# A gated delta-rule attention with a routed feed-forward: projections k, q, v, z as seven block products, four head groups, tiles of 512 tokens

## The chip, the cores and the metric

The kernel runs on one core of a Trainium2 chip. The metric is device time in microseconds; lower is better. Before the change it took 4070.05 us, the median of three runs (4065.21 to 4073.33).

## What is computed

Input x is 4 sequences of 1024 tokens with 512 features, all in f32. It is layer-normalised and goes two ways; the result is x + s * silu(ffn).

```
xn   = layernorm(x)
qkvz = xn @ w_qkvz.T            # 4096 tokens x 6144 rows: q, k 8 heads x 128; v, z 16 heads x 128
q, k, v = silu(causal_conv4([q, k, v]))      # four taps for each channel
beta, g = sigmoid(b), -exp(A_log) * softplus(a + dt_bias)
q, k = l2norm(q), l2norm(k)     # repeated for the two v heads of each k head
S = S * exp(g); S += k (beta * (v - k S)); o = (q * 128**-0.5) S     # for each token, S 128 x 128
s = (rmsnorm(o * silu(z)) * norm_weight) @ w_out.T
g = silu(where(routed, ffn(xn), xn))          # value/output product, gated mlp with 1408 columns
out = x + s * g
```

## The kernel before, in words

The program has two parts, one after the other. `feed_forward` works through 16 units of 256 tokens. It writes the normalised columns (channels on the partitions) to a scratch tensor in HBM, xt_scratch, and the decay rates and the feed-forward result to others. Its own products already use seven block products.

`attention` then goes through two groups of heads (4 k heads and 8 v heads each). In a group it goes through 4 sequences, and in each through 4 tiles of 256 tokens (32 tiles in all). A tile loads its columns into xtile (two buffers, with three tokens of the tile before, 259 columns) and makes its projections: `pe_product` (L1227) computes one feature of 128 channels in four matmuls over the contraction, weights as the stationary operand and 259 columns moving (L1239), or one z block of 512 columns with the tokens stationary (L1243). An f32 matmul stands in the trace as two records. Products and the score products share three PSUM banks in rotation (bank 0, 1, 3). ScalarE evicts a feature with the fourth tap (`act_lead`, L1262), VectorE adds the other three taps straight from the PSUM bank (`dve_conv`, L1269), and ScalarE takes the silu of four heads at once (L1282); z is evicted with its silu (L1277). Keys and queries are transposed in blocks of 32 by VectorE and through a scratch tensor in HBM, for their norms; keys go back the same way.

A chunk is 128 tokens, a unit is a chunk of one block of four v heads; there are 128 units. For each unit: scores (L1472, L1480), the decay matrix (L1489, L1497), its products with the scores (L1512, L1519), then an f16 triangular inverse in six levels with a correction (L1574 to L1690), which runs for two units side by side on two PSUM banks; then the recurrence: recall of the state, eps, learn, answer (L1699 to L1799), the gate with z and the rms norm (L1806 to L1832), a transpose through HBM, and the output product `pe_out` (L1888) into bank 2. The first group of heads stores its partial output in HBM, the second reads it back, adds its own and finishes.

The order of each engine's instructions is worked out before the program is built by `planned` (L980): a list scheduler over lanes of steps with prices from the table TAKES (L2113), dependences from `after` (L1992), and priority to the step with the longest path behind it. Each engine then runs its list in order and waits on semaphores. SP issues nearly all DMAs in such an order; ScalarE's queue issues the loads of xtile (L147), of decay rows (L142) and of the second group's weights.

Of the kernel before, what the change touches and what calls it, by code (L numbers as in the profile page):

```python
# [24 lines left out]
ALU = mybir.AluOpType  # L25
# [4 lines left out]
P = 128  # L30
# [6 lines left out]
GROUPS = 2  # L37
# [4 lines left out]
W_SPANS = {"k": (0, GK * P), "q": (GK * P, 2 * GK * P), "v": (2 * GK * P, (2 * GK + GV) * P), "z": ((2 * GK + GV) * P, GROWS)}  # L42
PADT = T + HALO
TILE = 256
CPT = TILE // P
WIN = TILE + HALO
# [9 lines left out]
HALF_TILES, HALF_CHUNKS = TILES // GROUPS, CHUNKS // GROUPS  # L56
# [49 lines left out]
def resident(nc, ctx):  # L106

    shapes = {"con": ([P, N_CONST, P], F32), "mask": ([P, N_MASK, P], F16), "nw": ([P, 1], F32), "wt": ([P, KT, GROWS], F32), "xtile": ([P, 2, KT, WIN], F32), "sel": ([P, 2, D], F32),
              "taps": ([P, GROUPS, 4 * GK, TAPS], F32), "gts": ([P, SLOTS, CPT, KINDS, GV], F32), "grows": ([P, 2, HEADS * P], F32)}
    r = {name: ctx.enter_context(nc.sbuf_tensor(name, shape, dtype)) for name, (shape, dtype) in shapes.items()}  # L110
    for name in ("c_in", "wk_in", "wq_in", "wv_in", "wz_in", "small_in", "x_in0", "x_in1", "g_out0", "g_out1", *(f"gt_in{i}" for i in range(SLOTS)), "gr_in0", "gr_in1"):
        r[name] = ctx.enter_context(nc.semaphore("a_" + name))
# [15 lines left out]

def load_weights(sp, r, w_qkvz, g, kind):
    lo, hi = W_SPANS[kind]  # L130
    sp.dma_start(r["wt"][:, :, lo:hi], w_qkvz[:, g * GROWS + lo:g * GROWS + hi].rearrange("(k p) n -> p k n", p=P)).then_inc(r[f"w{kind}_in"], 16)
# [13 lines left out]
def load_columns(sp, r, xt_d, q):  # L145
    b, i = divmod(q % HALF_TILES, TPB)
    sp.dma_start(r["xtile"][:, q % 2], xt_d[:, :, b * PADT + i * TILE:b * PADT + i * TILE + WIN]).then_inc(r[f"x_in{q % 2}"], 16)  # L147


def feed_forward(nc, bank, r, x, x_cols, stat_d, cst, masks, w_qkvz, w_ba, conv_w, dt_bias, a_log, norm_weight,  # L150
# [3 lines left out]
    with ExitStack() as ctx:  # L154
# [10 lines left out]
        both = r["wt"][:].rearrange("p k n -> p (k n)")  # L165
# [13 lines left out]
        KH, PIECES = KT // 2, (0, 3, 7, FT)  # L179
# [15 lines left out]
        o3 = r["xtile"][:, 1].rearrange("p k w -> p (k w)")[:, 256:256 + D].rearrange("p (k c) -> p k c", k=KH)  # L195
# [9 lines left out]
        spare, w = r["xtile"][:, 0].rearrange("p k w -> p (k w)"), NJ * NG  # L205
# [3 lines left out]
        gout = r["xtile"][:, 1].rearrange("p k w -> p (k w)")[:, 0:2 * KINDS * w].rearrange("p (t j g i h) -> p t j g i h", t=2, j=NJ, g=GROUPS, i=KINDS)  # L209
# [4 lines left out]
        names = ["c_in", "r_in", *(f"w_in{e}" for e in range(KT)), "g_in0", "g_in1", "g_in2", "d_in", "set", "z_out", "wvo_ps", "wvo_sb", "cb_ps", "at_sum",  # L214
# [80 lines left out]
        def dve_stats(dve, u):  # L295
            for j in range(NJ):
                dve.wait_ge(s[f"x_in{j}"], 16 * (u + 1))
                if u:
                    dve.wait_ge(s["mvs"], NJ * (u - 1) + j + 1)
# [2075 lines left out]
```

## Time and profile before

| | |
|---|---|
| runs | 4070.05 us median (4065.21 to 4073.33) |
| profiled execution, its own time | span of 4068.1 us from the first to the last instruction; no time around it is given |
| TensorE / VectorE / ScalarE / GpSimd busy | 98% / 77% / 56% / 36% |
| mean granted TensorE clock | 0.995 |
| DMA | 400.9 MB, mean 99 GB/s |

The profile is of one execution. Busy times are unions over time, so a line's busy time can hold the end of a matmul while the next one has started. "Idle before" a group is idle time of its engine, with what ended it.

### The profile page before, as it was taken

Reading aid. Unit: us, or ns where it says so; the run is one execution under the profiler, and the core shown is the slowest. Engines: PE = TensorE matmul, PEld = TensorE weight load, DVE = VectorE, ACT = ScalarE, POOL = GpSimd, SP = SyncE. Lnnn points to the kernel's source line nnn. Section 1 sums busy time; section 2 is a strip of 40 time slices with the busy share of each in tenths; the row PEclk is TensorE's granted clock in tenths of the full one; section 3 lists DMA queues with packets and bytes.
Section 4 is the critical chain, followed back from the end, with each engine's and each line's share of the span. In section 5 each row is a group of like instructions: output and inputs, shape, how many; then the busy total and the mean of one; then the engine's idle time right before and its main releaser. Section 6 shows DMA issues by size and latency. Waiting matters only on the chain. (4 is left out here: it accounts for less than half of the span.)

```text
span 4068.1 us, 83861 instructions
## 1 busy us (share of the span) xinstructions
PE 3999.3 (98%) x29432; PEld 3042.7 (75%) x29432; DVE 3147.1 (77%) x6660; ACT 2279.5 (56%) x5904; POOL 1482.6 (36%) x1744
## 2 busy tenths in 40 slices
PE   7999999999999999999999999999999999999998
PEld 6788787787777777777777777777777777777775
DVE  6766666665588878888888887788888888877885
ACT  2222222222277676666767666766666676666664
POOL 2322232322133334333333333334444444444445
PEclk9999999999999999999999999999999999999999
DMA  5212111110534344434434454444444444454443
GB/s 151 51 34 49 31 43 49 25 49 21 163 94 105 105 110 103 104 101 102 102 97 108 105 144 128 110 129 120 111 119 116 114 125 125 119 131 125 119 107 97
DMA packets 813539, 400.89 MB, mean 99 GB/s; under 512 B 475584, under 2 KB 738752, under 8 KB 813120
## 3 DMA queue, kind: packets, MB, share of 16 engines
q1 hardware_dynamic: 777024, 340.30, 32.1%
q10 hardware_dynamic: 36096, 55.24, 4.9%
q8 instruction: 234, 3.83, 0.4%
q14 instruction: 185, 1.52, 0.1%
HBM read 242.70 MB, written 152.63 MB: 97 GB/s over the span
## 5 line engine op out<-in xcount | busy, mean ns | idle before, releaser
L1239 PE MATMUL bank<-xtile,wt 128*128 128x259 f32 x4096 | 1073.2, 391 | 5.2 <-PEq L764 2.5
L1239 PEld LDWEIGHTS bank<-xtile,wt 128*128 128x128 f32 x4096 | 736.9, 191 | 148.7 <-issue 59.6
L1631 ACT ACTIVATE xyinv<-bank 128x512 f16<-128x512 f32 x768 | 451.7, 590 | 320.2 <-PE bank L1574 317.2
L1888 PE MATMUL bank<-wot,xnt 128*128 128x512 f32 x1024 | 537.6, 611 | 1.1 <-DVE xnt L1847 0.8
L1243 PE MATMUL bank<-wt,xtile 128*128 128x512 f32 x1024 | 521.1, 607 | 0.0
L1607 DVE TENSOR_TENSOR wlev<-bank,mask 128x256 f16<-128x256 f32 x768 | 316.8, 413 | 149.9 <-PE bank L1574 146.1
L548 PE MATMUL bank<-hb,wt 128*128 128x128 f32 x2816 | 376.4, 277 | 8.4 <-DVE part L588 5.7
L1269 DVE SCALAR_TENSOR_TENSOR vraw<-bank,taps,vraw 128x256 f32<-128x256 f32 x768 | 363.3, 476 | 27.3 <-ACT vraw L1262 13.5
L548 PEld LDWEIGHTS bank<-hb,wt 128*128 128x128 f32 x2816 | 350.2, 194 | 17.5 <-issue 7.2
L611 POOL TENSOR_TENSOR hid<-part 128x256 f32<-128x256 f32 x176 | 139.0, 790 | 474.2 <-ACT part L603 474.2
L1574 PEld LDWEIGHTS bank<-xyinv,lth 128*128 128x128 f16 x3584 | 202.1, 98 | 146.2 <-issue 71.6
L1549 POOL TENSOR_TENSOR kend<-ktok,gts 128x256 f32<-128x256 f32 x224 | 136.9, 632 | 464.6 <-issue 464.3
L625 PE MATMUL bank<-wd_sb,hid 128*128 128x512 f32 x704 | 304.8, 592 | 0.0
L1524 POOL TENSOR_TENSOR ltm<-ltm,mask 128x512 f32<-128x512 f32 x128 | 154.7, 1209 | 399.2 <-DVE ltm L1512 399.2
L548 PE MATMUL bank<-hb,comb 128*128 128x128 f32 x2112 | 295.9, 277 | 0.0
L1806 POOL TENSOR_TENSOR tq<-tq,zs 128x512 f32<-128x512 f32 x128 | 175.2, 1369 | 326.6 <-DVE tq L1799 308.5
L1574 PE MATMUL bank<-xyinv,lth 128*128 128x64 f16 (+1 forms) x3584 | 264.0, 197 | 18.0 <-ACT xyinv L1631 15.9
L548 PEld LDWEIGHTS bank<-hb,comb 128*128 128x128 f32 x2112 | 266.9, 194 | 0.0
L1243 PEld LDWEIGHTS bank<-wt,xtile 128*128 128x128 f32 x1024 | 178.1, 191 | 118.1 <-issue 114.8
L1574 PEld LDWEIGHTS bank<-wlev,xyinv 128*128 128x128 f16 x3072 | 169.9, 98 | 127.5 <-issue 87.6
L603 ACT ACTIVATE part<-part 128x256 f32<-128x256 f32 x176 | 73.4, 417 | 332.0 <-DVE part L598 332.0
L625 PEld LDWEIGHTS bank<-wd_sb,hid 128*128 128x128 f32 x704 | 132.5, 190 | 160.7 <-issue 157.1
(217 smaller groups left out, 8609.8 us busy)
## 6 DMA issues: line engine op xcount, KB each, us to landing
v_scratch<-vraw SPq DMA_DIRECT2D x64, 512.0 KB, 3.3
vtok<-v_scratch SPq DMA_DIRECT2D x512, 64.0 KB, 2.2
x_scratch<-tq SPq DMA_DIRECT2D x508, 64.0 KB, 1.8
xnt<-x_scratch SPq DMA_DIRECT2D x508, 64.0 KB, 2.5
grows<-row_scratch ACTq DMA_DIRECT2D x126, 256.0 KB, 3.7
k_scratch<-kraw SPq DMA_DIRECT2D x32, 512.0 KB, 2.6
ktok<-k_scratch SPq DMA_DIRECT2D x256, 64.0 KB, 2.5
b_scratch<-kraw SPq DMA_DIRECT2D x256, 64.0 KB, 1.8
```

The source lines that it names most:

```text
L548: i = pe.matmul(dst, w[:, k, f * P:(f + 1) * P], b[:, k], start=first and k == 0, stop=k == KH - 1, skip_group_check=True)
L611: pool.tensor_tensor(hid[:, f, :].rearrange("p (t c) -> p t c", t=2), part[:, n % 3, 0:2], part[:, n % 3, 2:4], ALU.mult).then_inc(s["hid_ ...
L625: i = pe.matmul(bank[6 + j % 2][:], hid[:, f, j * P:(j + 1) * P], wd_sb[:, f, :], start=(f == 0), stop=(f == FT - 1))
L1239: j = pe.matmul(b_p[:, 0:WIN], wt[:, k, c:c + P], xtile[:, par, k, :], **st)
L1243: j = pe.matmul(b_p[:], xtile[:, par, k, HALO + cc * P:HALO + (cc + 1) * P], w, **st)
L1269: dve.scalar_tensor_tensor(out=acc, in0=shaped(feats[i][0], tile_bank("product", q, prod_of[i])[:, tap:tap + TILE]), scalar=taps[:, group( ...
L1524: pool.tensor_tensor(ltm[:], ltm[:], mask[:, M_NEG, :].unsqueeze(1).broadcast_to([P, HEADS, P]), ALU.subtract).then_inc(s["lti_sb"], 1)
L1574: i = pe.matmul(dst[:, h * cols:(h + 1) * cols], lhsT(h), rhs(h), start=start and h == 0, stop=stop, skip_group_check=True)
L1607: dve.tensor_tensor(wlev[:, lv - 1].rearrange("p h (b t s) -> p h b t s", t=2, s=z)[:, :, :, 0, :], b_inv[p][:, 0:HEADS * P // 2].rearrang ...
L1631: act.activation(dst, b_inv[p][:].rearrange("p (a h b s) -> p a h b s", a=2, h=HEADS, s=z), ACT.Copy).then_inc(s[f"xy_sb{p}"], 1)
L1806: pool.tensor_tensor(tq[:, n % 2], tq[:, n % 2], zs[:, tile % 2, cc, m], ALU.mult).then_inc(s["xf_sb"], 1)
L1888: i = pe.matmul(b_o[:], xnt[:, h], wot[:, h], start=(h == 0), stop=(h == GV - 1))
```

## The change

The groups of heads become four (2 k heads, 4 v heads each), the tiles 512 tokens, so there are again 32 tiles and 128 units, and a unit is a chunk. The projections of a tile are three quads: k and q, v, z. A quad is a product of 512 weight columns, 512 tokens and 512 channels, cut into 2 x 2 blocks of 256 each way, and made by seven products of blocks in place of eight; each of the seven is four matmuls with 256 moving columns. Four sums of weight blocks are formed once a group and kind (VectorE for the first group, GpSimd for the others), four sums of column blocks once a tile (VectorE for the first tile, GpSimd for the others). A quad uses all three rotating banks: P1, P6, P7, P4 accumulate in one, and after each ScalarE copies the bank to one quarter of the result; P2 and P5, P3 go to the other two, and VectorE adds those to the copies. For k, q and v the result stands in an SBUF line, `stage`, of 3 + 512 tokens; GpSimd copies the three tokens of the tile before into it and keeps the last three. The lead tap on ScalarE and three taps on VectorE then read that line, with 512 columns each. z is copied to its place and gets its silu there. The score product moves to bank 2, which the output product uses as well: the scores of unit n wait for the eviction of output n - 4, and output c waits for the scores of unit c + 3.

Columns of a tile come in four DMAs and weights of a kind in four, both now from SP. Partial outputs are stored and read back for three groups (96 chunks). Keys and queries are loaded back in 4 DMAs each and not 8. The zero padding of xt_scratch goes, and several semaphores of the feed-forward part are merged.

```diff
-GROUPS = 2
+GROUPS = 4
-TILE = 256
+TILE = 512
+QUADS = ("kq", "v", "z")
 def load_columns(sp, r, xt_d, q):
-    b, i = divmod(q % HALF_TILES, TPB)
-    sp.dma_start(r["xtile"][:, q % 2], xt_d[:, :, b * PADT + i * TILE:b * PADT + i * TILE + WIN]).then_inc(r[f"x_in{q % 2}"], 16)
+    at = q % GROUP_TILES * TILE
+    for slot, k, side in ((B11, 0, 0), (B21, 1, 0), (B12, 0, 1), (B22, 1, 1)):
+        sp.dma_start(r["xtile"][:, q % 2, slot], xt_d[:, k * KH:(k + 1) * KH, at + side * HTILE:at + (side + 1) * HTILE]).then_inc(r[f"x_in{q % 2}"], 16)
...
+        PX, PY, PW = ("P1", "P6", "P7", "P4"), ("P2",), ("P5", "P3")
+        OPERANDS = {"P1": (A11, B11), "P2": (A12, B21), "P3": (S4, B22), "P4": (A22, T4), "P5": (S1, T1), "P6": (S2, T2), "P7": (S3, T3)}
+        COPIED = ("C11", "C12", "C22", "C21")
+        ADDED = ("C11", "C22", "C12")
...
+        def sum_weights(engine, g, kind):
+            engine.tensor_tensor(w[:, S1], w[:, A21], w[:, A22], ALU.add).then_inc(s["wsum"], 1)
+            engine.wait_ge(s["wsum"], done + 1)
+            engine.tensor_tensor(w[:, S3], w[:, A11], w[:, A21], ALU.subtract).then_inc(s["wsum"], 1)
+            engine.tensor_tensor(w[:, S2], w[:, S1], w[:, A11], ALU.subtract).then_inc(s["wsum"], 1)
+            engine.wait_ge(s["wsum"], done + 3)
+            engine.tensor_tensor(w[:, S4], w[:, A12], w[:, S2], ALU.subtract).then_inc(s["wsum"], 1)
+        def sum_columns(engine, q):
...
+        def pe_quad(pe, t, p, r):
+            b = x_bank(t) if p in PX else y_bank(t) if p in PY else w_bank(t)
+            if r == 0:
+                if p == "P1":
+                    pe.wait_ge(s[f"x_in{par}"], 64 * (q // 2 + 1))
+                    pe.wait_ge(s[f"w{kind}_in"], 64 * (group(q) + 1))
+                    if t:
+                        pe.wait_ge(s["qa_sb"], 3 * (t - 1) + 1)
+                elif p == "P2":
+                    if t:
+                        pe.wait_ge(s["qa_sb"], 3 * t)
+                elif p == "P5":
+                    pe.wait_ge(s["xsum"], 4 * (q + 1))
+                    pe.wait_ge(s["wsum"], 4 * (group(q) * NQ + j + 1))
+                    if t:
+                        pe.wait_ge(s["qc_sb"], 4 * t)
+                elif p == "P3":
+                    pe.wait_ge(s["qa_sb"], 3 * t + 2)
+                else:
+                    pe.wait_ge(s["qc_sb"], 4 * t + PX.index(p))
+            for k in range(KH):
+                if kind == "z":
+                    lhs, rhs = xtile[:, par, right, k, r * P:(r + 1) * P], wt[:, left, k, lo:lo + QCOLS]
+                else:
+                    lhs, rhs = wt[:, left, k, lo + r * P:lo + (r + 1) * P], xtile[:, par, right, k, :]
+                i = pe.matmul(b[:, r * QCOLS:(r + 1) * QCOLS], lhs, rhs, start=p in FIRST and r == 0 and k == 0, stop=k == KH - 1, skip_group_check=True)
...
+        def wait_place(engine, t, part):
+            m = staged(q, j)
+            if m:
+                engine.wait_ge(s["cv"], HALO * side_done(m - 1, side))
+                if half:
+                    engine.wait_ge(s["edge"], edges(m))
...
+        def act_copy(act, t, i):
+            act.activation(target(t, part), pairs(x_bank(t)), ACT.Silu if last_z else ACT.Copy).then_inc(s["qc_sb"], 1)
+        def dve_add(dve, t, i):
+            dve.tensor_tensor(a, pairs(y_bank(t) if part == "C11" else w_bank(t)), a, ALU.add).then_inc(s["qa_sb"], 1)
+        def pool_halo(pool, m):
+                pool.tensor_copy(stage[:, :, :, 0:HALO], tails[:, j]).then_inc(s["edge"], 1)
+        def pool_tail(pool, m):
+            pool.tensor_copy(tails[:, j], stage[:, :, :, TILE:TILE + HALO]).then_inc(s["edge"], 1)
...
         def act_lead(act, q, i):
-            act.activation(feature(q, i), shaped(kind, tile_bank("product", q, prod_of[i])[:, HALO:HALO + TILE]), ACT.Copy, scale=taps[:, group(q), i, HALO:HALO + 1]).then_inc(s["lead"], 1)
+            act.activation(feature(q, i), shaped(kind, stage[:, side, r, HALO:HALO + TILE]), ACT.Copy, scale=taps[:, group(q), f, HALO:HALO + 1]).then_inc(s["lead"], 1)
         def dve_conv(dve, q, i, tap):
-            dve.scalar_tensor_tensor(out=acc, in0=shaped(feats[i][0], tile_bank("product", q, prod_of[i])[:, tap:tap + TILE]), scalar=taps[:, group(q), i, tap:tap + 1], in1=acc,
-                                     op0=ALU.mult, op1=ALU.add).then_inc(s[done[tap + 1]], 1)
+            dve.scalar_tensor_tensor(out=acc, in0=shaped(feats[i][0], stage[:, side, r, tap:tap + TILE]), scalar=taps[:, group(q), f, tap:tap + 1], in1=acc,
+                                     op0=ALU.mult, op1=ALU.add).then_inc(s["cv"], 1)
...
+        def act_zsilu(act, q, part):
+            act.activation(a, a, ACT.Silu).then_inc(s["zs_sb"], 1)
...
         def pe_scores(pe, n):
+            if n > LEAD:
+                pe.wait_ge(s["po_sb"], n - LEAD)
...
         def pe_out(pe, c, h):
+                pe.wait_ge(s["kq_sb"], min(c + LEAD + 1, UNITS))
...
+        def product_order():
+            yield 0, "P1"
+            for t in quads:
+                yield from ((t, p) for p in (("P5", "P2", "P6", "P7") if QUADS[t % NQ] == "v" else ("P5", "P6", "P2", "P7")))
+                if t + 1 in quads:
+                    yield t + 1, "P1"
+                yield from ((t, p) for p in ("P4", "P3"))
...
-            ("act", "lead"): 0.47, ("act", "z"): 0.60, ("act", "silu"): 1.06, ("act", "keys"): 1.27, ("act", "queries"): 1.27,
+            ("act", "lead"): 0.64, ("act", "zsilu"): 0.85, ("act", "silu"): 1.06, ("act", "keys"): 1.27, ("act", "queries"): 1.27,
-            ("dve", "conv"): 0.50,
+            ("dve", "conv"): 0.64,
```

## Rows read from the trace of the kernel before

**Rows 1.** The page: busy us, share of span, instructions, by engine.
```profile
PE 3999.3 (98%) x29432; PEld 3042.7 (75%) x29432; DVE 3147.1 (77%) x6660; ACT 2279.5 (56%) x5904; POOL 1482.6 (36%) x1744
```

**Rows 2.** Busy time by stage: bounds, length, engines busy, granted clock, DMA.
```profile
0.00:1061.00 1061.00, 1036.56 (x6644) 840.42 (x6644) 684.81 (x1691) 254.56 (x599) 299.91 (x402) 0.99 0.20 56
1061.00:1200.00 139.00, 130.25 (x779) 96.30 (x780) 109.51 (x209) 80.75 (x202) 32.97 (x36) 0.96 0.40 112
1200.00:4003.00 2803.00, 2783.32 (x21657) 2074.78 (x21656) 2326.02 (x4707) 1922.50 (x5036) 1126.12 (x1279) 1.00 0.44 114
4003.00:4068.00 65.00, 49.17 (x360) 31.15 (x356) 26.73 (x56) 21.64 (x68) 23.61 (x28) 0.92 0.32 81
```

**Rows 3.** The same for VectorE alone, then for the taps of line 1269.
```profile
1061.00:4003.00 2942.00, 2435.53 (x4914) 1.00 0.44 114
1061.00:4003.00 2942.00, 725.11 (x1536) 1.00 0.44 114
```

**Rows 4.** Lines by shape: the products; busy us, mean ns, idle before.
```profile
L1239 PE MATMUL bank<-xtile,wt 128*128 128x259 f32 x4096 | 1073.2, 391 | 5.2 <-PEq L764 2.5 <-DVE vraw L1269 1.4 <-DVE kqt L1269 1.0
L1243 PE MATMUL bank<-wt,xtile 128*128 128x512 f32 x1024 | 521.1, 607 | 0.0
```

**Rows 5.** Timeline of ScalarE at the start: start, duration, line, idle before.
```profile
1066.67 0.47 ACT L1262 ACTIVATE kraw<-bank,taps 128x256 f32<-128x256 f32 x1 [1.22 <-PE bank L1239]
...
1068.43 0.47 ACT L1262 ACTIVATE kraw<-bank,taps 128x256 f32<-128x256 f32 x1 [1.28 <-PE bank L1239]
...
1101.78 0.60 ACT L1277 ACTIVATE zs<-bank 128x512 f32<-128x512 f32 x1 [2.84 <-PE bank L1243]
...
1105.21 0.60 ACT L1277 ACTIVATE zs<-bank 128x512 f32<-128x512 f32 x1 [2.84 <-PE bank L1243]
```

**Rows 6.** VectorE by line: ns min/median/max, first and last start.
```profile
L1519 DVE TENSOR_TENSOR pt<-gam,kqm x128: 647/682/1764, 1118.7 to 4003.2; 128x512 f32<-128x512 f32 x128
L526 DVE SCALAR_TENSOR_TENSOR h<-h,routed,xn x32: 750/751/1097, 106.4 to 993.2; 128x512 f32<-128x512 f32 x32
L1799 DVE TENSOR_TENSOR tq<-bank,tq x112: 673/684/693, 1203.0 to 4050.5; 128x512 f32<-128x512 f32 x112
L1653 DVE TENSOR_TENSOR errh<-errd,mask x128: 398/415/1370, 1154.9 to 4039.1; 128x512 f16<-128x512 f16 x128
```

**Rows 7.** Lines by shape: two operations with two SBUF inputs.
```profile
L1519 DVE TENSOR_TENSOR pt<-gam,kqm 128x512 f32<-128x512 f32 x128 | 109.9, 859 | 1.0 <-PE bank L1786 1.0
L1653 DVE TENSOR_TENSOR errh<-errd,mask 128x512 f16<-128x512 f16 x128 | 69.6, 544 | 0.0
```

**Rows 8.** Timeline of GpSimd and VectorE in one stretch of attention.
```profile
2522.82 1.15 POOL L1524 TENSOR_TENSOR ltm<-ltm,mask 128x512 f32<-128x512 f32 x1 [9.85 <-DVE ltm L1512]
2523.26 1.00 DVE L1653 TENSOR_TENSOR errh<-errd,mask 128x512 f16<-128x512 f16 x1
```

**Rows 9.** Lines by shape: ScalarE and GpSimd.
```profile
L1262 ACT ACTIVATE vraw<-bank,taps 128x256 f32<-128x256 f32 x256 | 118.9, 468 | 92.1 <-PE bank L1239 90.8
L1532 ACT ACTIVATE lth<-ltm 128x512 f16<-128x512 f32 x128 | 80.5, 629 | 23.0 <-POOL ltm L1524 23.0
L1282 ACT ACTIVATE vraw<-vraw 128x1024 f32<-128x1024 f32 x64 | 67.6, 1056 | 16.0 <-DVE vraw L1269 15.5
L1524 POOL TENSOR_TENSOR ltm<-ltm,mask 128x512 f32<-128x512 f32 x128 | 154.7, 1209 | 399.2 <-DVE ltm L1512 399.2
```

**Rows 10.** DMA issues: line, count, size, us to landing.
```profile
xtile<-xt_scratch ACTq DMA_DIRECT2D x30, 518.0 KB, 4.3
```

**Rows 11.** Timeline at the start of attention: VectorE.
```profile
1061.54 1.76 DVE L1125 CAST wlev<-con 128x512 f16<-128x512 f32 x5
```

**Rows 12.** Timeline: one inverse's start and end.
```profile
2520.61 0.42 DVE L1595 TENSOR_TENSOR xyinv<-lth,mask 128x512 f16<-128x512 f16 x1
...
2561.56 0.69 DVE L1690 SCALAR_TENSOR_TENSOR yfin<-bank,xyinv 128x512 f32<-128x512 f32 x1 [0.76 <-PE bank L1574]
```

More of the change, by code:

```diff
@@ L1423, in load_values @@
+        def load_values(sp, q, cc):
+            n, half = q * UPT + cc, cc // HCH
+            sp.wait_ge(s[f"v_o{half}"], 16 * (q + 1))
             if q:
@@ L1982, in attention @@
-        lane("act tile", (a for step in turns for a in evictions(*step) if a[0] == "act"))
-        lane("dve tile", (a for step in turns if step[0] != "scores" for a in evictions(*step) if a[0] == "dve"))
-        lane("act keys", (("act", "keys", q, cc) for q in tiles for cc in range(CPT)))
-        lane("act queries", (("act", "queries", q, cc) for q in tiles for cc in range(CPT)))
+        lane("pool out", (("pool", "out", c) for c in chunks[LAST_ROWS:]))
+        quads = range(NQ * TILES)
@@ new lines, in attention @@
+        halves = range(HALVES)
+        def product_order():
[5 more added lines that the diff above has]
+                yield from ((t, p) for p in ("P4", "P3"))
+        lane("pe tile", (("pe", "quad", t, p, r) for t, p in product_order() for r in range(2)))
+        lane("pe scores", (("pe", "scores", n) for n in units))
@@ new lines, in attention @@
+        lane("act copy", (("act", "zlast" if i == 3 and QUADS[t % NQ] == "z" else "copy", t, i) for t in quads for i in range(4)))
+        lane("dve add", (("dve", "add", t, i) for t in quads for i in range(3)))
+        lane("act conv", (("act", "lead", q, i) for q in tiles for i in range(NF)))
+        lane("dve conv", (("dve", "conv", q, i, tap) for q in tiles for i in range(NF) for tap in range(HALO)))
+        lane("pool halo", (("pool", what, m) for m in range(STAGED * TILES) for what in ("halo", "tail") if what == "halo" or m // STAGED % TPB == 0))
@@ new lines, in attention @@
+        lane("act zsilu", (("act", "zsilu", q, part) for q in tiles for part in range(2)))
+        lane("pool xsum", (("dve" if q == 0 else "pool", "xsum", q) for q in tiles))
+        lane("wsum", (("dve" if g == 0 else "pool", "wsum", g, j) for g in range(GROUPS) for j in range(NQ)))
+        lane("sp xin", (("sp", "xin", q) for q in tiles[2:]))
+        lane("sp weights", (("sp", "pload", g, j) for g in range(1, GROUPS) for j in range(NQ)))
+        lane("act keys", (("act", kind, q, half) for q in tiles for kind in ("keys", "queries") for half in halves))
@@ L2005, in after @@
+            if at == ("pe", "scores"):
+                tile = where(n)[2]
+                return [("dve", "scores", n - 1), ("dve", "out", n - LEAD - 1), ("sp", "bload", tile, HALVES - 1), ("act", "silu", tile, 1)]
             last = (n - 1) * UPT - 1
             if at == ("act", "lead"):
[L2007 to L2009 removed]
@@ L2010, in after @@
-                return [("pe", "product", n, prod_of[i[1]], KT - 1)] + first
+                (what, h), (side, _), j = feats[i[1]], place_of(i[1]), i[1] // 4
+                t = n * NQ + j
+                first = {"k": [("pe", "recall", last), ("pe", "scores", last)], "q": [("pe", "query", last), ("pe", "scores", last), ("dve", "queries", n - 2)],
+                         "v": [("sp", "vstore", n - 1, half) for half in range(HALVES)]}[what] if h == 0 else []
+                return [("pool", "halo", staged(n, j))] + ([("dve", "add", t, 1), copied(t, 3)] if side else [("dve", "add", t, 0), ("dve", "add", t, 2)]) + first
```

718 lines of the change are left out of this document (405 added, 313 removed).

## The prediction

> **What bounds the kernel now.** I read the engine shares first, then the busy time by stage, then the lines, then the timeline. TensorE is busy for 98% of the span, VectorE for 77% [rows 1]. By stage: the feed-forward part ends at 1061 us and the change hardly touches it; the attention part from 1200 to 4003 us has TensorE busy for 2783 of 2803 us, that is idle for 20 us, at the full granted clock; the last 65 us are a drain [rows 2]. So attention is paid by TensorE's work, and VectorE stands behind it with 2435.5 of the 2942 us from 1061 to 4003, or 83% [rows 3]. Busy time of TensorE counts modelled ends that overlap the next start, so I price its work by the pace at which results come. The profiled span is 4068.1 us; the median of the runs is 4070.05, so about 2 us lie around the span, and I carry them over.
>
> **TensorE: the products.** The k, q and v products are 4096 records of 259 columns, that is 2048 matmuls in two passes each, and z is 1024 records of 512 columns [rows 4]. At the start of attention nothing else runs: a feature of eight passes comes every 1.755 us (1066.67, 1068.43), so a pass of 259 columns takes 0.219 us; a z block of eight passes comes every 3.43 us (1101.78, 1105.21), so a pass of 512 columns takes 0.429 us [rows 5]. Before: 4096 x 0.219 + 1024 x 0.429 = 897 + 439 = 1336 us. After: 32 tiles x 3 quads x 7 products x 2 halves x 2 k-blocks = 2688 matmuls, 5376 passes of 256 columns. The line through the two paces gives 0.83 ns a column and 4 ns fixed, so 0.2166 us for 256 columns: 1164 us. The saving is 172 us (by columns alone, seven eighths and 256 for 259, it would be 175). The other work of TensorE is the same in count: 128 units before (64 chunks, two blocks of heads) and after (128 chunks, one block), 512 out matmuls, as many scores, recalls, levels.
>
> **VectorE.** Removed: 1536 taps of 256 columns read from PSUM, 725 us [rows 3]. Added: 768 taps of 512 columns, both inputs in SBUF; 288 additions of 512 columns from PSUM; 16 sums at the start. The additions are priced by the row of the same form, 0.684 us (L1799): 197 us. The sums, at 0.69 us each, 11 us. The trace has no such tap in attention. Nearest rows: a tensor-tensor operation of 512 columns with two SBUF inputs has median 0.682 and minimum 0.647 us; the scalar-tensor-tensor form in the feed-forward part has 0.751 [rows 6]. But the mean of the first is 0.859 us, 0.177 above its median; that of errh is 0.544 over 0.415, 0.129 above [rows 6, 7], while operations that read PSUM stay within 20 ns of theirs (L1799 has 693 at most). The timeline shows why: errh, started at 2523.26, took 1.00 us instead of 0.41 and ended only after the GpSimd operation of 2522.82 with its 1.15 us [rows 8]. So moving the taps from PSUM to SBUF exposes them to GpSimd. I take 0.69 + 0.14 = 0.83 us a tap: 637 us; bounds 0.647 (497 us) and 0.751 + 0.177 = 0.93 (714 us). Sum: 2435 - 725 + 637 + 197 + 11, and 20 more for the old two-input operations, which meet a busier GpSimd: 2575 us; the bounds are 2415 and 2652.
>
> The Trainium skill's page "SBUF — State Buffer", section "SBUF: two separate sides", says that a VectorE operation with two SBUF inputs and a GpSimd operation that reads SBUF take an exclusive lock, and that the loser blocks fully. Errh above agrees. It speaks against this change, and what it could make of the time, worked out from rows, is the second rival below.
>
> **ScalarE.** Removed: 512 leads at 0.468 us (240 us) and 128 z evictions (76 us). Added: 384 evictions at 0.597 (229 us), 256 leads of 512 columns at 0.629 (161 us), 32 silus of 512 and 32 of 1024 columns (19 + 34 us): +127 us [rows 5, 9]. ScalarE had 1922 of 2803 us [rows 2]; it goes to about 76%, and TensorE covers it, unless its queue delays a copy that a quad waits for. If none of that cover held, +127 us; below nothing it can't go. I take nothing by itself, and put the queueing into the stall below.
>
> **GpSimd.** Sums of columns for 31 tiles and of weights for nine quads, 160 operations at 1.209 us, 193 us [rows 9]; and 96 tiny copies, under 30 us. From 40% of the steady stage to about 51%. It sits in the inverse's preparation, but GpSimd stood idle for VectorE before ltm for 399 us [rows 9], so by itself nothing, up to 20 us.
>
> **DMA.** Columns are read four times and not twice (each tile load is 518 KB before, 4.3 us to land [rows 10]), now as four DMAs on SP instead of one on ScalarE's queue; partial sums are stored and reloaded 96 times, not 32. Together some 50 MB, on engines at 44% [rows 2]; key and query loads are halved in number. SP gets 120 issues for columns and 36 for weights ahead of whatever is queued, and loses 256. A tile's load is released a whole tile (some 88 us) before its use. I take nothing; from -5 to +15 us. Wot is now loaded three times behind the last out of a group; out is delayed for a dozen us and other work covers it.
>
> **The start.** Only P1 can run before the column and weight sums. VectorE first fills its constants until 1063.3 [rows 11], then makes 4 + 4 chained sums of 0.69 us, some 5.5 us, and P1 covers 1.7: about 6 us. The first keys come only after a whole quad (12 us, where the first features of k took 7), and products of this and the next tile cover most of that. I take +8, from 0 to +20.
>
> **The stall.** What is late next once 172 us are gone? The steady stage now idles 20 us, with VectorE at 83%. VectorE would now stand at 2575 / 2828 = 91%. The order is written ahead by a planner that prices a tap at 0.64 and knows nothing of the blocking, so 768 x 0.19 = 146 us of VectorE's time is not in its plan. And the filler is less loose: formerly each feature waited only for its own bank; now a quad holds all three banks, P6, P7 and P4 each wait for a copy, and the next staged quad waits until nine taps have read the line. I take 70 us of idle time for 20: +50, from 0 to +130 (at +130 the stage would be 2908 us and VectorE, at its upper 2652 us, 91% of it, so that it sets the pace).
>
> **Sum.** 4070 - 172 + 8 + 50 = 3956; I say 3955.
>
> **Rivals.** (1) Full gain: blocking is rare and the plan holds; 4070 - 172 + 0 to 8 gives 3898 to 3906. For it: today's 0.7% idle in spite of 83%. Against: the surplus of 0.13 to 0.18 us in today's rows.
> (2) VectorE becomes the bound through the blocking. A GpSimd operation in the stage lasts 1126 / 1279 = 0.88 us [rows 2] and one is running half of the time; if every tap that meets one waits for half of it or more, and back-to-back taps alternate with GpSimd, a tap costs 0.93 us, and VectorE's total is 2652 + 25 us. At 92% busy the stage is 2910 us and not 2942: 4070 - 32 + 8 = 4046. For it: rows 7 and 8. Against: GpSimd is often idle just when the taps run.
> (3) Slower: the chain of quads through the one line. Per tile: three quads, each 4 products on one bank (6.9 us), 4 copies (2.4), an addition (0.7) and 9 hand-overs of w, and 9 taps at a pace s before v may fill the line: 3 x (10 + 9w) + 9s. It decides from 2942 / 32 = 91.9 us a tile, as with w = 1.5 and s = 2.4; at w = 1.6 and s = 2.4 it is 94.8 us, 32 times that is 3034, and the time 4070 + 92 + 8 = 4170. Against it: the inverse's chain, from its start at 2520.61 to its end at 2561.56 [rows 12], holds some 35 operations with 14 us of own work, so 27 / 35 = 0.77 us a hand-over; with s = 1.5 that is 64 us a tile, and 88 are there. For it: the planner puts the inverse ahead, and the quads may get what is left.
>
> **Chances.** Forecast, 3910 to 4015: 0.56. Full gain: 0.13. VectorE bound, up to 4062: 0.15. Slower by the chain or by a mixture of it and VectorE: 0.13. The rest, 0.03, lands on no change. A measurement of this kernel tells about 0.2% (8 us) from nothing. Faster 0.83, same 0.04, slower 0.13. The range, 3888 to 4080, leaves out the far part of rival 3 and a gain beyond the counted one; the forecast's own is 3910 to 4015.
>
> **What would show it.** Right: 5376 records of 256 columns; the mean of a tap between 0.75 and 0.90 us with maxima above 1.5; VectorE above 88% of the steady stage; TensorE idle 50 to 100 us in it, released mostly by VectorE and by ScalarE's copies; first scores some 10 us later. Wrong: taps at 0.65 with no spread (then rival 1); TensorE idle above 150 us with VectorE under 88%, released by the copies and additions (rival 3); a fall of the granted clock in the steady stage, which no term here holds.

## The result, and the profile after

The change made the kernel slower: 4445.84 us (median, 4440.69 to 4452.78) against 4069.23 us (4065.21 to 4073.33), a ratio of 1.092 with a 95% interval of 1.090 to 1.094. The prediction said 3955, and its range ended at 4080. The profiled execution spans 4438.9 us, with a mean granted clock of 0.952 where it was 0.995.

The page of the kernel after, busy time by engine, answers to [rows 1]:

```profile
PE 4027.7 (91%) x29688; PEld 3205.8 (72%) x29688; DVE 3351.7 (76%) x6260; ACT 2328.1 (52%) x5908; POOL 1800.7 (41%) x2000
```

The same by stage, with the columns of [rows 2] (length, then busy time of PE, PEld, DVE, ACT and POOL, then granted clock, DMA share, GB/s). The first stage is not shown: it has 1035.97 us of PE work in 1061, as before.

```profile
1061.00:1200.00 139.00, 110.35 (x673) 90.96 (x674) 108.37 (x161) 71.14 (x173) 42.70 (x42) 0.85 0.32 88
1200.00:4368.00 3168.00, 2833.34 (x22044) 2244.08 (x22045) 2528.27 (x4350) 1981.19 (x5069) 1430.22 (x1525) 0.95 0.44 119
4368.00:4438.00 70.00, 48.00 (x330) 30.64 (x328) 29.42 (x60) 21.33 (x69) 28.34 (x32) 0.84 0.31 87
```

The steady stage grew from 2803 to 3168 us. Two things are in it. TensorE is idle for 335 us (3168 - 2833) where it was idle for 20. And its busy time rose by 50 us where the prediction took 172 us off, so 222 us of busy time are there that the count of passes doesn't explain. Some 20 of them are only shifted work: the start stage has 110 us of TensorE work where it had 130. Over the whole span the extra is 4027.7 - 3999.3 + 172 = 200 us. VectorE is at 80% of the stage (2528 / 3168), less than its 83% of before: no engine is full, and every one waits.

That the work itself came out as counted is in the lines, by shape (busy, mean ns, idle before). Products first, to be held against [rows 4]:

```profile
L1294 PE MATMUL bank<-xtile,wt 128*128 128x256 f32 x3584 | 956.5, 403 | 36.3 <-ACT stage L1325 17.1 <-DVE zs L1336 8.0 <-DVE wt L1248 6.9
L1294 PE MATMUL bank<-wt,xtile 128*128 128x256 f32 x1792 | 455.3, 388 | 1.8 <-ACT zs L1325 1.5
```

Their busy time is 1412 us where the rows of before add up to 1594: 182 us less. (Busy time counts overlapping records: in the trace of after a pass's record lasts 0.379 us in the median, and the next one starts 0.216 us after it.) Then VectorE's taps, additions and two old operations with both inputs in SBUF (pt is L1519 of before, errh L1653, [rows 7]):

```profile
L1386 DVE SCALAR_TENSOR_TENSOR vraw<-stage,taps,vraw 128x512 f32<-128x512 f32 x384 | 319.3, 843 | 12.6 <-ACT vraw L1379 7.0
L1386 DVE SCALAR_TENSOR_TENSOR kqt<-stage,taps,kqt 128x512 f32<-128x512 f32 x384 | 317.7, 837 | 5.7 <-ACT kqt L1379 1.7
L1654 DVE TENSOR_TENSOR pt<-gam,kqm 128x512 f32<-128x512 f32 x128 | 142.1, 1110 | 0.0
L1336 DVE TENSOR_TENSOR stage<-bank,stage 128x512 f32<-128x512 f32 x192 | 130.9, 682 | 87.7 <-PE bank L1294 59.6 <-ACT stage L1325 27.1
L1788 DVE TENSOR_TENSOR errh<-errd,mask 128x512 f16<-128x512 f16 x128 | 65.0, 508 | 0.0
```

What TensorE waited for is in the waits (engine and line that waited, who released it: us in total, times, longest):

```profile
PE bank L1709 <- DVE wlev L1742: 80.9, 95, 2.6
PE bank L1709 <- ACT xyinv L1766: 63.3, 64, 3.2
PE bank L1709 <- DVE xyinv L1736: 47.4, 36, 5.6
PE bank L1709 <- DVE errl L1812: 45.1, 44, 3.9
PE bank L1294 <- ACT stage L1325: 17.1, 17, 5.8
```

These are whole-span totals, in which TensorE is idle for 411 us (69 before). The inverse (L1709), whose steps depend on one another, has 269 us of them by its rows. The products (L1294) have 38 us in all. Before, the rows of this chain (L1574) have 28 us of idle time; I take it that work which was free to start filled its gaps, and that now this work often can't start. The timeline of one longer gap shows how (start, duration, engine, line, and in brackets the idle time before it):

```profile
2077.67 2.20 POOL L1659 TENSOR_TENSOR ltm<-ltm,mask 128x512 f32<-128x512 f32 x1 [8.83 <-DVE ltm L1647]
2077.86 1.96 PE L2023 MATMUL bank<-wot,xnt 128*128 128x512 f32 x4
2078.77 3.99 DVE L1386 SCALAR_TENSOR_TENSOR kqt<-stage,taps,kqt 128x512 f32<-128x512 f32 x3
...
2080.37 0.29 PE L1709 MATMUL bank<-xyinv,lth 128*128 128x64 f16 x4
2080.91 1.31 POOL L1673 TENSOR_TENSOR ltl<-ltm,lth 128x512 f16<-128x512 f32 x1 [1.04 <-ACT lth L1667]
2082.69 1.23 DVE L1421 STREAM_TRANSPOSE kraw<-kqt 128x1024 f32<-128x1024 f32 x1
2082.86 0.60 ACT L1325 ACTIVATE stage<-bank 128x512 f32<-128x512 f32 x1 [2.02 <-DVE kqt L1386]
2083.85 0.65 DVE L1812 SCALAR_TENSOR_TENSOR errl<-bank,xyinv 128x512 f16<-128x512 f32 x1
2084.55 0.58 PE L1709 MATMUL bank<-errl,errh 128*128 128x128 f16 x4 [3.89 <-DVE errl L1812]
2084.76 0.67 DVE L2037 TENSOR_TENSOR prow<-bank,prow 128x512 f32<-128x512 f32 x1
2084.93 2.02 PE L1294 MATMUL bank<-xtile,wt 128*128 128x256 f32 x4
2086.74 0.63 PE L1607 MATMUL bank<-kqt 128*128 128x256 f32 x1
```

Three taps take 3.99 us, 1.33 each, beside two GpSimd operations that read SBUF. ScalarE's copy of the next quad (L1325) stood still for 2.02 us until the last of them had read the one line. Behind the taps stands errl, which the inverse needs. TensorE has nothing that may start: the product's bank waits for that copy, which is done at 2083.46 (from then on the product stands behind the inverse in TensorE's list), and the scores (2086.74) stand in bank 2 behind the output of 2077.86, which VectorE evicts only at 2084.76. So it is idle for 3.89 us. The granted clock around this gap and another, and in the gap and right behind it (same columns as the stages):

```profile
2050.00:2060.00 10.00, 6.68 (x46) 5.34 (x46) 5.42 (x11) 2.16 (x4) 8.90 (x9) 0.87 0.53 171
2070.00:2080.00 10.00, 9.94 (x77) 6.89 (x73) 9.96 (x16) 8.56 (x18) 2.20 (x1) 1.00 0.40 98
2080.00:2090.00 10.00, 6.02 (x42) 5.02 (x41) 8.64 (x12) 2.09 (x5) 1.31 (x1) 0.83 0.43 139
2080.00:2084.50 4.50, 0.57 (x8) 0.28 (x6) 4.43 (x6) 1.43 (x3) 1.31 (x1) 1.00 0.01 4
2084.60:2088.00 3.40, 3.40 (x11) 2.79 (x12) 2.56 (x5) 0.00 (x0) 0.00 (x0) 0.50 0.69 253
```

The clock is 1.00 (2.4 GHz) from 2070 us to the end of the gap, and 0.50 (1.2 GHz) right behind it, where TensorE is busy again all the time. So the low level falls on work, not on the gap.

One more wait is in the trace of after, on GpSimd, which also prepares the inverse's operands. Before its column sums it stands for the load of the columns:

```profile
POOL xtile L1258 <- DMA xtile<-xt_scratch: 171.6, 27, 13.2
```

Whether this delays the inverse was not tested by itself.

### The profile page after: what moved, and what is told of

Same layout as the page of the kernel before. It is cut to its first block and busy times, and to the rows that moved or that the text cites. A ratio compares the mean times of both kernels' runs of the same rounds, so it can differ in the third digit from the quotient of the medians.

```text
span 4438.9 us, 85469 instructions
## 1 busy us (share of the span) xinstructions
PE 4027.7 (91%) x29688; PEld 3205.8 (72%) x29688; DVE 3351.7 (76%) x6260; ACT 2328.1 (52%) x5908; POOL 1800.7 (41%) x2000
## 5 line engine op out<-in xcount | busy, mean ns | idle before, releaser
L1294 PE MATMUL bank<-xtile,wt 128*128 128x256 f32 x3584 | 956.5, 403 | 36.3 <-ACT stage L1325 17.1
L1294 PEld LDWEIGHTS bank<-xtile,wt 128*128 128x128 f32 x3584 | 675.1, 199 | 179.6 <-issue 77.9
L1294 PE MATMUL bank<-wt,xtile 128*128 128x256 f32 x1792 | 455.3, 388 | 1.8 <-ACT zs L1325 1.5
L1742 DVE TENSOR_TENSOR wlev<-bank,mask 128x256 f16<-128x256 f32 x768 | 307.9, 411 | 175.0 <-PE bank L1709 173.1
L1294 PEld LDWEIGHTS bank<-wt,xtile 128*128 128x128 f32 x1792 | 326.4, 191 | 63.1 <-issue 24.6
L1659 POOL TENSOR_TENSOR ltm<-ltm,mask 128x512 f32<-128x512 f32 x128 | 179.7, 1404 | 470.5 <-DVE ltm L1647 470.4
L1709 PEld LDWEIGHTS bank<-xyinv,lth 128*128 128x128 f16 x3584 | 204.5, 101 | 221.9 <-issue 93.4
L1709 PE MATMUL bank<-xyinv,lth 128*128 128x64 f16 (+1 forms) x3584 | 259.5, 202 | 112.6 <-ACT xyinv L1766 63.3
L1386 DVE SCALAR_TENSOR_TENSOR vraw<-stage,taps,vraw 128x512 f32<-128x512 f32 x384 | 319.3, 843 | 12.6 <-ACT vraw L1379 7.0
L1386 DVE SCALAR_TENSOR_TENSOR kqt<-stage,taps,kqt 128x512 f32<-128x512 f32 x384 | 317.7, 837 | 5.7 <-ACT kqt L1379 1.7
L1709 PEld LDWEIGHTS bank<-wlev,xyinv 128*128 128x128 f16 x3072 | 173.4, 101 | 179.9 <-DVE wlev L1742 120.3
L1709 PE MATMUL bank<-wlev,xyinv 128*128 128x64 f16 x3072 | 222.2, 198 | 81.8 <-DVE wlev L1742 80.9
L1684 POOL TENSOR_TENSOR kend<-ktok,gts 128x256 f32<-128x256 f32 x224 | 148.9, 684 | 329.6 <-issue 329.2
```

The lines of the kernel that those rows point to most:

```text
L1294: i = pe.matmul(b[:, r * QCOLS:(r + 1) * QCOLS], lhs, rhs, start=p in FIRST and r == 0 and k == 0, stop=k == KH - 1, skip_group_check=True)
L1386: dve.scalar_tensor_tensor(out=acc, in0=shaped(feats[i][0], stage[:, side, r, tap:tap + TILE]), scalar=taps[:, group(q), f, tap:tap + 1], ...
L1659: pool.tensor_tensor(ltm[:], ltm[:], mask[:, M_NEG, :].unsqueeze(1).broadcast_to([P, HEADS, P]), ALU.subtract).then_inc(s["lti_sb"], 1)
L1684: i = pool.tensor_tensor(kend[:, r * REP:(r + 1) * REP].rearrange("p r (a x) -> p r a x", a=NBLK), ktok[:, tile % 2, :, cc, m * KPB + r].u ...
L1709: i = pe.matmul(dst[:, h * cols:(h + 1) * cols], lhsT(h), rhs(h), start=start and h == 0, stop=stop, skip_group_check=True)
L1742: dve.tensor_tensor(wlev[:, lv - 1].rearrange("p h (b t s) -> p h b t s", t=2, s=z)[:, :, :, 0, :], b_inv[p][:, 0:HEADS * P // 2].rearrang ...
```

## Experiments

Theory A: the waits' structure makes the idle time. Bank 2 forces a strict alternation of scores and outputs with `LEAD = 3` units between them, and the one line and the three banks of a quad make a second loop; the clock falls as a consequence. The rivals: the taps out of SBUF, lengthened by GpSimd, and VectorE with them (B); the prices of the planner (C). The letters in the texts on record are each text's own.

**How far scores run ahead.** The kernel after, with one number changed, in both directions:

```diff
-        LEAD = 3
+        LEAD = 5        (e1; 2 in e2)
```

> The changed kernel with LEAD = 5 in place of 3: the scores of unit n wait for the eviction of output n - 6, and output c for the scores of unit c + 5. Nothing else is changed. Theory A (the loop through bank 2 holds a unit's whole latency within four units, TensorE idles, and its clock falls for it): 4150 us (4080 to 4220), TensorE idle in attention down from 386 us to some 250, mean granted clock up from 0.952 to 0.97 or more, taps still 0.80 to 0.86 us. Theory B (the taps' reads from SBUF and GpSimd's new work make VectorE late; the bank is no matter): 4400 to 4446 us, idle and clock as before.

> The changed kernel with LEAD = 2. Theory A: slower in proportion to the tighter loop, 4790 us (4650 to 4900), TensorE idle in attention above 550 us and mean clock below 0.93. Theory B: within 1% of 4446 us.

Measured: 4275.1 us with 5 (ratio to before 1.049, 1.048 to 1.051) and 4710.75 us with 2 (1.157, 1.156 to 1.159). The steady stages, of 5 and then of 2:

```profile
1200.00:4206.00 3006.00, 2763.79 (x22074) 2189.39 (x22072) 2526.73 (x4354) 1942.76 (x5063) 1457.00 (x1527) 0.97 0.46 124
```

```profile
1200.00:4639.00 3439.00, 2948.76 (x22174) 2283.63 (x22172) 2535.96 (x4366) 1960.14 (x5061) 1434.06 (x1529) 0.92 0.41 110
```

With 2 the time is in A's range (4650 to 4900); with 5 it is 55 us above the end of A's (4080 to 4220), so the distance gives less than A expected. From 2 to 3 the time falls by 265 us, from 3 to 5 by 171; VectorE's busy time in the stage stays within 10 us, and the taps don't get shorter (means of 843 and 837 ns, then 879 and 833 with 5). So 171 of the 377 us lost hang on the distance in bank 2, with the taps' reads and GpSimd's work left as they are.

**Two lines.** `stage` gets a second buffer, one for k and q and one for v, so that a quad waits for the taps of the quad before the last. For the room, z is kept in f16 and the separate tails go; these two are part of what e3 measures.

```diff
-        stage, tails = sb("stage", [P, 2, 2, HALO + TILE]), sb("tails", [P, 2, 2, 2, HALO])
+        stage = sb("stage", [P, 2, 2, 2, HALO + TILE])
-            if m:
-                engine.wait_ge(s["cv"], HALO * side_done(m - 1, side))
+            if m >= 2:
+                engine.wait_ge(s["cv"], HALO * side_done(m - 2, side))
```

> LEAD stays 3. Two SBUF lines, one for the quad of k and q and one for v, so that a staged quad's copies wait for the taps of the quad before the last and no longer for those of the last; the three tokens of halo are copied within a line and the tails buffer goes. To make room the silu of z is kept in f16. Theory A': the single line is a second loop of this kind: 4210 us (4130 to 4300), TensorE idle down from 386 to some 270 us. Theory B: within 1% of 4446 us, since the reads and GpSimd's work are the same. If only bank 2 binds: also within 1%.

> Both: two lines and LEAD = 5. Theory A with A': 4060 us (4000 to 4150), TensorE idle under 200 us in attention, mean clock 0.98 or more. If the two loops are one (either cure gives it all): no better than the better of the two alone.

Measured: 4264.67 us with `LEAD = 3` (1.047, 1.044 to 1.050) and 4198.49 us with both edits (1.032, 1.029 to 1.034). The second line alone gives 181 us, about as much as the distance alone; together they give 247, less than the 352 of the two added up. I take it that each lets the products or the scores fill gaps that the other also fills; no run shows this by itself. e3 is in its range, e4 is 48 us above the end of A's (4150): the two loops together are not the whole loss.

**The coupling alone, in the kernel before.** Nothing of Strassen; only the order that the shared bank forces.

```diff
+        LEAD = 3
         def pe_scores(pe, n):
+            if n > LEAD + 1:
+                pe.wait_ge(s["po_sb"], (n - LEAD) // NB)
...
         pe.wait_ge(s["po_sb"], c)
+        pe.wait_ge(s["kq_sb"], min(NB * c + NB + LEAD, UNITS))
```

> The kernel before, no Strassen, its banks, line-free taps and products as they were. Added is only the order that the shared bank 2 forces after the change: the scores of unit n wait until the outputs of the units up to n - 4 are evicted, and output c waits for the scores three units beyond it; the plan of the orders is told of it. Theory A (this coupling alone costs, because a unit's way from scores to output is longer than three periods of about 22 us): 4120 to 4210 us, TensorE idle in 1200 to 4003 us grows from 20 to between 80 and 200 us, with levels, merges and eps as what it waits for, and the granted clock of the stage stays at or just under 1.00. Rival B (the coupling is harmless by itself and hurts only together with the single line and the three banks that a quad holds): within 20 us of 4070.

Measured: 4172.24 us (1.026, 1.024 to 1.027), 103 us more than before. Its steady stage:

```profile
1200.00:4105.00 2905.00, 2824.46 (x21651) 2082.45 (x21648) 2319.61 (x4705) 1861.18 (x4982) 1133.33 (x1279) 0.99 0.43 111
```

81 us idle and 103 us lost, both in A's ranges (the idle time at its lower edge), and against the rival: the coupling costs by itself. Why can be counted in the traces: the records of the scores (4 a unit) and of the output (16 a chunk, that is 8 a unit) that started before 2500 us (count, durations, first and last start). The kernel before:

```profile
L1472 PE MATMUL bank<-kqt x248: 377/379/483, 1106.7 to 2484.9; 128*128 128x256 f32 x124
L1888 PE MATMUL bank<-wot,xnt x426: 590/592/1061, 1199.0 to 2496.5; 128*128 128x512 f32 x142
```

and e9:

```profile
L1476 PE MATMUL bank<-kqt x240: 377/379/483, 1106.9 to 2490.9; 128*128 128x256 f32 x120
L1893 PE MATMUL bank<-wot,xnt x448: 590/592/1061, 1187.7 to 2486.6; 128*128 128x512 f32 x150
```

Before, 62 units had been scored and 53 had gone out: scores ran 9 units ahead when nothing bound them to the output (7 to 9.5 at other times of the stage). In after it is 55 and 51, the 4 that the coupling allows. In e9, where outputs go by chunks of two units, it is 60 and 56, and between 3 and 5 at other times.

**Taps from SBUF alone, in the kernel before.** e5 is a control: ScalarE also copies each feature's bank to an SBUF line, which nobody reads. In e6 the taps read it.

```diff
+            act.activation(line[:, n % 3], tile_bank("product", q, prod_of[i])[:, 0:WIN], ACT.Copy).then_inc(s["lead"], 1)
... e6 in addition:
-            in0=shaped(feats[i][0], tile_bank("product", q, prod_of[i])[:, tap:tap + TILE])
+            in0=shaped(feats[i][0], line[:, n % 3, tap:tap + TILE])
```

> The kernel before, where ScalarE also copies each feature's bank (259 columns) into an SBUF line that nobody reads: 512 more evictions of some 0.46 us. It is the control of the next run. All theories: ScalarE has the room (56% busy), 4070 to 4090 us.

> The same, and VectorE's 1536 taps read that SBUF line in place of the PSUM bank; the banks, loops, tiles and products are those of the kernel before. Theory A (the loops cost the time): a tap's mean goes from 0.472 to some 0.55 us with maxima above 1.5, VectorE to some 87%, and the time stays within 1% of the control, 4075 to 4120 us. Theory B (reads from SBUF against GpSimd make the loss): 4200 us or more.

Measured: 4085.64 us (1.004, 1.002 to 1.006) and 4178.08 us (1.027, 1.025 to 1.028), so the other input costs 92 us, between what A and B had. The taps of v in e5 and then in e6 (count, minimum/median/maximum in ns):

```profile
L1274 DVE SCALAR_TENSOR_TENSOR vraw<-bank,taps,vraw x768: 435/483/486, 1079.8 to 3935.5; 128x256 f32<-128x256 f32 x192
```

```profile
L1274 DVE SCALAR_TENSOR_TENSOR vraw<-line,taps,vraw x768: 437/485/1443, 1079.2 to 4032.1; 128x256 f32<-128x256 f32 x192
```

Minimum and median are the same; the maximum moves, from 486 to 1443 ns, and with it the mean, from 478 to 585. So an SBUF input isn't slower in itself: some taps are held up for most of a microsecond. All taps together cost 901 us (445 + 243 + 213) where e5 has 727: 174 us more of VectorE's time made the kernel 92 us longer, at a granted clock of 1.00. That a tap is held up by GpSimd is what the Trainium skill says in "SBUF — State Buffer", section "SBUF: two separate sides" (a VectorE operation with two SBUF inputs and a GpSimd operation that reads SBUF exclude each other for the whole instruction); the trace agrees, with the three taps at 2078.77 above.

**Less GpSimd.** e8 is e4 with GpSimd's column sums on 8 of 256 columns from the third tile on (the rest of the sums is left out).

```diff
+            if q >= 2:
+                w = w[:, :, :, 0:8]
```

> Two lines and LEAD = 5, and GpSimd's sums of the columns take 8 columns in place of 256 from the third tile on, so their result is not the sums; waits and order stay. Takes some 150 us of work off GpSimd's queue (51% to 45% busy). Theory A: within 1% of 4198. Theory B (GpSimd's new work blocks VectorE and holds its own queue up): taps fall from 0.87 to 0.80 us or less, and the time to 4130 us or below.

Measured: 4175.85 us (1.027, 1.025 to 1.029), 23 less than e4, though GpSimd lost 123 us (1805.8 to 1682.9). The taps' mean went from 884 to 863 ns (v). So the sums hold the taps up only a little, as A had it.

**The planner's prices.** Two lines and `LEAD = 5`, and prices nearer to the trace of after (e7); the same prices in the kernel after as it is (e10).

```diff
-("dve", "conv"): 0.64   ("dve", "attend"): 0.69  ("dve", "lower"): 0.69
+("dve", "conv"): 0.78   ("dve", "attend"): 0.9   ("dve", "lower"): 0.8
-("pool", "unit"): 1.16  ("pool", "xsum"): 4.9    ("sp", "xin"): 1.8
+("pool", "unit"): 1.4   ("pool", "xsum"): 5.7    ("sp", "xin"): 4.0
```

Not all of them are the trace's means: a tap has 0.84 us there and gets 0.78, attend (pt) has 1.11 and gets 0.9, lower has 0.87 and gets 0.8; unit (1.40), the column sums (5.66 for four) and the column load (3.9) fit.

> Two lines and LEAD = 5, and the planner's prices as the trace of the changed kernel measured them: tap 0.78 for 0.64, attend 0.9 for 0.69, lower 0.8 for 0.69, unit 1.4 for 1.16, column sums 5.7 for 4.9, the column load 4.0 for 1.8. Only the order of the instructions changes. If the written order is late because it underprices VectorE, 4198 falls to 4150 us (4120 to 4175); if what is left is the blocking itself and the structure, within 0.5% of 4198.

> The changed kernel with one line and LEAD = 3 as it is; only the planner's prices are replaced by what the trace of after shows (a tap 0.78, attend 0.9, lower 0.8, GpSimd unit 1.4 and column sums 5.7, column loads 4.0). It parts the prices from the structure. Theory A (the two loops hold the idle time, a better order can't get round them): 4380 to 4460 us, that is a gain of at most 65 us of the 376 lost, idle time above 300 us and a granted clock of at most 0.96 in the steady stage. Rival C (the wrong prices are the cause, as e7's gain of 68 us behind the loosened loops could suggest): 4330 or less.

Measured: e7 4130.68 us (1.015, 1.014 to 1.017), 68 less than e4, the best version with seven products that was found; e10 4398.01 us (1.082, 1.078 to 1.085), 48 less than after. Both times are in the range of a theory: e7 in that of an order that is late for its prices, e10 in A's (its idle time, 298 us, is just under the 300 that A gave). Prices matter, but without the looser loops they recover 48 of 377 us: C falls as the main cause. The runs change all prices at once, so they don't say which one counts. Steady stage of e7, then of e10:

```profile
1200.00:4058.00 2858.00, 2705.02 (x22015) 2155.81 (x22012) 2513.47 (x4352) 1950.55 (x5066) 1446.88 (x1495) 0.98 0.50 130
```

```profile
1200.00:4325.00 3125.00, 2826.84 (x22081) 2246.76 (x22081) 2506.97 (x4356) 1983.03 (x5085) 1431.36 (x1528) 0.94 0.45 120
```

**A tap less.** e7 with the last tap of every feature cut to 32 or 128 columns; the rest of that tap is left out.

```diff
+            if tap == HALO - 1:
+                acc, line = acc[:, 0:1], line[:, 0:1]
```

> The kernel of e7 (two lines, LEAD = 5, measured prices) with the same written order, but the last tap of every feature works on the first 32 or 128 of its 512 columns; the rest of that tap is left out, so 256 operations of 0.85 us become about 0.1 us and VectorE loses some 190 us of work. Rival B (VectorE, lengthened by SBUF taps, is what sets the pace of the rest): at least 100 us less than e7, 4030 or below. Theory A (what is left is the dependent chains of the inverse and the quads; VectorE only delays single links of them): 20 to 80 us less, 4050 to 4110, with the granted clock at 0.985 or above.

Measured: 4079.53 us (1.003, 1.001 to 1.004), 51 less than e7. VectorE was 88% busy in e7's stage (2513 / 2858), the share that the prediction gave as its sign; it lost 112 us of work (3338.0 to 3226.0 in the span), and 51 came back as time. It lost 112 and not 190 because the short taps took 0.40 us in the mean (375 ns for 32 columns, 434 for 128), and not 0.1. The ranges of both theories were made for 190 us: scaled to 112, A ends at 47 us and B starts at 59, and 51 lies between. So VectorE's work counts for about half of its length here. It doesn't set the pace alone, or all 112 us would have come back; it isn't a side matter either.

**Idle time, busy time and clock.** From the steady stage of every run; clocks are rounded; "extra" is TensorE's busy time over the 2783 us of [rows 2], or over 2783 - 172 = 2611 with seven products:

| | stage | idle | extra busy | clock |
|---|---|---|---|---|
| before | 2803 | 20 | 0 | 1.00 |
| e5 control copy | 2815 | 29 | 3 | 1.00 |
| e9 coupling alone | 2905 | 81 | 41 | 0.99 |
| e6 taps from SBUF | 2905 | 87 | 35 | 1.00 |
| e11 a tap less | 2812 | 125 | 76 | 0.99 |
| e7 prices, lines, 5 | 2858 | 153 | 94 | 0.98 |
| e8 short sums | 2898 | 183 | 104 | 0.98 |
| e4 two lines, 5 | 2931 | 198 | 122 | 0.98 |
| e3 two lines | 2986 | 225 | 150 | 0.97 |
| e1 `LEAD = 5` | 3006 | 242 | 153 | 0.97 |
| e10 prices | 3125 | 298 | 216 | 0.94 |
| after | 3168 | 335 | 222 | 0.95 |
| e2 `LEAD = 2` | 3439 | 490 | 338 | 0.92 |

In the kernels with seven products the extra is 0.6 to 0.7 of the idle time, whatever made the idle time. With the shifted work of the start taken out, over whole spans and against the 69 us of idle time of before, it is 0.5 to 0.65 us for each added microsecond (after: 200 for 342; e7: 84 for 148; e2: 308 for 506).

How much of it is the clock can be bounded by the trace's record of the granted clock. In after's steady stage the clock stands at 1.2 GHz for 348 us in 50 stretches (7 us in two stretches in the stage of before), and TensorE is busy for 272 us of them. Over the whole span, work at the low level (a product pass starts every 0.427 us there in the median) can have cost 141 us more than before, half of its length, so at most 141 of the 200 us are the clock. The other 60 or so go with the number of idle gaps, 411 more than before: 0.15 us a gap. In the other runs the same rest is 0.14 to 0.26 us a gap (e7: 42 of 84 for 216 gaps; e6, whose clock costs 5 us less than that of before: 43 for 166). That is about what the last pass before a gap lasts beyond its place in the row (0.379 - 0.216 = 0.16 us for 256 columns). This part stays an estimate: the profile models the ends of matmuls, and no run changed the number of gaps alone.

## Why the prediction was wrong

**Terms that held.** The passes: 5376 of 256 columns. The product rows lost 182 us of busy time, for a forecast of 172. The pace of a pass is 0.216 us, as forecast. The taps: 637 us forecast, 319.3 + 317.7 = 637.0 measured, with a mean of 0.84 for 0.83 and a maximum over 1.5 (1.83). That it is so exact is luck: the forecast took a base of 0.69 us and 0.14 for GpSimd, and the median came out at 0.74 to 0.75 us, with 0.09 above it. The additions: 197 us forecast, 130.9 + 65.0 = 195.9 measured. TensorE waited 6.9 us for the weight sums (L1248), 6 forecast.

**Smaller misses.** VectorE from 1061 us to the end of the steady stage: 2637 us, where 2575 was forecast and 2652 was the upper bound. The start: TensorE is idle for 29 us between 1061 and 1200 us where it was idle for 9, that is 20 us for a forecast of 8, the end of that term's range. The columns' load, taken as nothing: GpSimd waited 172 us for it. GpSimd, 1801 us against 1483 before: +318, where 193 + 30 were forecast: the sums took 230 and the small copies 19, and its old operations got some 70 us longer (ltm: 1404 ns for 1209), which was missed.

**The step that failed** is "The stall": "I take 70 us of idle time for 20: +50, from 0 to +130". It measured 335 us of idle time in the steady stage, that is +315. It was sized mainly by how full VectorE would be (91%), and VectorE came out less full (80%) than before (83%). What made the idle time was who waits for whom. Of the three things that made it, two were named in words and priced too low, and one wasn't named:
- Bank 2, shared by scores and output. The prediction counted the scores' work and didn't price their new place, though the wait was in the diff. e9 prices it alone at +103 us; in the changed kernel, loosening it gives back 171 (e1) and tightening it by one costs 265 (e2). It could be counted in the trace of before: its scores run 9 units ahead of the output, and the diff allows 4. A unit takes about 2803 / 128 = 21.9 us, so the diff leaves 88 us from a unit's scores to its output, where before there were 9 units' time, some 190 us; one inverse takes 41 of the 88 (2520.61 to 2561.56, [rows 12]).
- The one line. Rival 3 had this mechanism, with 3 x (10 + 9w) + 9s a tile, and put it at 0.13. A second line gives back 181 us (e3). Rival 3 was the nearest of the three, but its own sum, 4170, was 276 us short, for it let that chain set the pace alone. Of its sign half came (idle above 150 us, VectorE under 88%) and half didn't: the copies and additions hold the products up for 38 us at most, and the waits of the inverse are 269. In the excerpt the line acts together with bank 2, by leaving a gap of the inverse unfilled.
- VectorE's queue. The taps, three in a row and now up to 1.83 us each, stand before errl and wlev, which the inverse waits for. This is where contention enters: 92 us in the kernel before (e6). What it costs in the changed kernel no run parts from the rest.

**The missing term** is what idle time costs beyond itself. The prediction held the granted clock at 1.00 and the busy time at the count of passes, and named a fall of the clock as what would prove it wrong. Measured, this term is 200 us over the span. The two account for the miss: TensorE is idle for 411 us of the span, where the sum had 69 + 8 + 50 = 127, that is +284, and the extra busy time is +200, together 484 of the 490 us between 3956 and 4446. e7 closes the same way: 216 - 127 = 89, and 84, together 173, against the 175 us by which it lies over the forecast.

**What is open.** No version with seven products beat the kernel before; e7 is 1.5% above it. The extra 200 us divide into at most 141 for the clock and a rest that follows the number of gaps; the second is an estimate. The wait of GpSimd for the columns is 172 us in after, 118 in e4, 88 in e7 and 186 in e10, so it goes along with the gain in some runs and not in all; a run that loads the columns earlier and changes nothing else is missing. A bank of its own for the scores wasn't tried, since the three rotating banks, two of the inverse and two of the recurrence leave none. The effects aren't additive (e1 and e3), so no share of the 377 us belongs to one cause alone.

## What to carry to other kernels

When a change takes a resource away (a bank shared by two stages, one line for three producers), count in the trace how far the two sides run apart today and compare that with the distance which the new wait allows, before any sum of busy times (here 9 units against 4); an engine at 98% busy is held there by filler work that is free to start, and the change may take that freedom. Count added idle time on TensorE at 1.5 to 1.7 times its length in a kernel of this kind. And give a list scheduler prices from the trace of the changed kernel, contention and loads included: here that was worth 48 to 68 us for no other edit.

## What the runs showed of the hardware

The granted clock went down with the idle time, from 1.00 at 0.7% and at 3.0% idle (before, e6) to 0.95 at 10.6% and 0.92 at 14.3% (after, e2), though not by the sum alone: e9, with 2.8% idle, has 0.99 and e6, with 3.0%, 1.00. e6 has many short gaps (the longest 2.8 us), e9 fewer and longer ones (up to 5.2 us). It didn't take long gaps either: of the 50 stretches at 1.2 GHz in after's steady stage, 45 had no gap of 3 us in the 5 us before them; the longest there was 0.5 to 2.8 us. The Trainium skill, "TensorE: Matmul & The Clock Gate", section "A second HAM failure mode: psum-queue depth-cycling", says of a bf16 kernel that short idles between groups of matmuls that cycle through PSUM banks make the clock swing between its two levels. The trace agrees with the swing: 50 stretches at the low level in the steady stage, 348 us, where the kernel before has two.

A tap from SBUF has the same minimum and median as one from PSUM (437 and 485 ns against 435 and 483), and the difference is in the held-up ones: a maximum of 1443 for 486, a mean of 585 for 478 (e6, e5). And the price of contention seems to move with the order of the instructions: pt has a mean of 1110 ns in after, 852 in e7, while errh goes from 508 to 720, with nearly the same work on both engines:

```profile
L1653 DVE TENSOR_TENSOR pt<-gam,kqm 128x512 f32<-128x512 f32 x128 | 109.1, 852 | 0.0
L1787 DVE TENSOR_TENSOR errh<-errd,mask 128x512 f16<-128x512 f16 x128 | 92.2, 720 | 0.0
```
